# Attention of a four-layer block: the product with V in two halves, and steps of GpSimd, ScalarE and the queues set to other places

## What is computed

```
b, s, _ = x.shape                       # 4, 1024; x is layer-normed before
ids = _adapter_ids(lora_start_indices, b)
Q = _multilora(x, ids, Wq, Aq, Bq)      # x Wᵀ + (x Aᵀ) Bᵀ, by the batch's adapter
K = _multilora(x, ids, Wk, Ak, Bk)
V = _multilora(x, ids, Wv, Av, Bv)
Q, K, V = (split(Q), split(K), split(V))   # 16 heads of 16
Q, K = (_rope(Q), _rope(K))
scores = jnp.einsum('bhqd,bhkd->bhqk', Q, K) / jnp.sqrt(16)
scores = jnp.where(causal, scores, -jnp.inf)
attn = jax.nn.softmax(scores, axis=-1)
out = jnp.einsum('bhqk,bhkd->bhqd', attn, V)
out = out.transpose(0, 2, 1, 3).reshape(b, s, D_MODEL)
return _multilora(out, ids, Wo, Ao, Bo)
```

## Time and profile before

| | us |
|---|---|
| three timed runs | 2107.85, 2112.87, 2113.27 |
| median | 2112.87 |
| the profiled execution, its own time | 2114.4 |
| its span | 2112.7 |
| TensorE, matrix products busy | 1789.8 |
| TensorE, weight loads busy | 1186.0 |
| VectorE busy | 1277.1 |
| ScalarE busy | 864.4 |
| GpSimd busy | 714.8 |

### The profile page before, as it was taken

How to read it: one execution, slowest core, us unless ns; L and a number is a source line. 1 busy time by engine, 2 the same in 40 slices (tenths; PEclk the granted TensorE clock), 3 DMA queues, 4 the chain that set the end, 5 groups by cost and what they waited for, 6 DMA issues and landing times. The chain is left out here.

```text
span 2112.7 us, 30095 instructions
## 1 busy us (share of the span) xinstructions
PE 1789.8 (85%) x9549; PEld 1186.0 (56%) x9549; DVE 1277.1 (60%) x3120; ACT 864.4 (41%) x1791; POOL 714.8 (34%) x873
## 2 busy tenths in 40 slices
PE   5478888889788884799999768989898966999998
PEld 4133333334333333588888635748384745888886
DVE  5476677667676705755555456665766667555554
ACT  2146555556565654122222135553645550222221
POOL 2326344463454421232322123333242321223231
PEclk9669989989997797799999969998999987999999
DMA  5624343342534624376676540110202043767674
GB/s 159 211 66 125 98 140 106 110 132 86 159 97 149 213 80 186 142 259 245 249 255 240 185 175 1 60 41 1 100 1 101 1 181 135 254 240 261 238 258 169
DMA packets 103462, 312.23 MB, mean 148 GB/s; under 512 B 23304, under 2 KB 54796, under 8 KB 93200
## 3 DMA queue, kind: packets, MB, share of 16 engines
q1 hardware_dynamic: 86016, 257.08, 34.5%
q0 software_dynamic: 15936, 50.35, 7.6%
q10 hardware_dynamic: 1360, 2.89, 0.4%
HBM read 245.12 MB, written 53.87 MB: 142 GB/s over the span
## 5 line engine op out<-in xcount | busy, mean ns | idle before, releaser
L772 ACT ACTIVATE a_probs<-a_ps_e 128x512 f32<-128x512 f32 (+3 forms) x768 | 335.9, 491 | 200.8 <-PE a_ps_e L947 196.8
L511 DVE CUSTOM_DVE_ANT_0 a_ps_m<-a_ps_m,a_causal 128x512 f32<-128x512 f32 (+3 forms) x512 | 239.5, 517 | 114.0 <-PE a_ps_m L934 113.1
L1445 ACT CAST hidden_high<-g_ps_h 128x512 fp32r<-128x512 f32 x140 | 75.2, 589 | 400.9 <-PE g_ps_h L1590 400.9
L947 PE MATMUL a_ps_e<-a_q_st,a_k_st 64*128 64x512 f32 (+3 forms) x768 | 185.6, 474 | 60.1 <-ACT a_probs L772 49.0
L947 PEld LDWEIGHTS a_ps_e<-a_q_st,a_k_st 64*128 64x128 f32 x768 | 79.0, 199 | 268.0 <-ACT a_probs L772 190.6
L515 DVE TENSOR_REDUCE a_peak<-a_ps_m 128x1 f32<-128x512 f32 x256 | 164.6, 685 | 102.8 <-PE a_ps_m L934 102.0
L963 PE MATMUL a_ps_a<-a_probs,a_vals 128*32 128x512 f32 (+3 forms) x1536 | 185.9, 560 | 17.3 <-issue 17.1
L934 PE MATMUL a_ps_m<-a_k_st,a_q_st 64*128 64x512 f32 (+3 forms) x768 | 153.5, 401 | 50.1 <-DMA a_k_st<-a_scr_k 23.5
L653 POOL TENSOR_SCALAR_AFFINE_SELECT a_probs<-a_probs 128x256 f32<-128x256 f32 x256 | 103.4, 407 | 270.1 <-ACT a_probs L772 269.1
L111 POOL TENSOR_TENSOR g_xe_rs<-g_xe_ve,table 128x1 f32<-128x1 f32 x70 | 39.3, 561 | 442.9 <-DVE g_xe_ve L1286 442.9
L1578 PE MATMUL g_ps_y<-g_w_d,hidden_high 128*128 128x512 f32 x560 | 143.4, 398 | 5.9 <-DVE x_res L1322 5.9
(11 more groups left out here) (298 smaller groups left out, 3822.8 us busy)
## 6 DMA issues: line engine op xcount, KB each, us to landing
g_w_d<-down_rows SPq DMA_DIRECT2D x70, 2048.0 KB
a_q_st<-a_scr_q POOLq DMA_DIRECT2D x32, 512.0 KB, 4.0
a_k_st<-a_scr_k POOLq DMA_DIRECT2D x32, 512.0 KB, 4.8
m_spread_acs<-m_acs_rows SPq DMA_DIRECT2D x8, 2048.0 KB, 9.6
a_scr_q<-a_high SPq DMA_DIRECT2D x34, 256.0 KB
a_scr_k<-a_high SPq DMA_DIRECT2D x32, 256.0 KB
a_swapped<-a_raw SPq DMA_DIRECT2D x64, 128.0 KB, 2.0
g_x_rows<-x_res SPq DMA_DIRECT2D x8, 1024.0 KB, 12.0
```

What stands on the lines that cost most here:

```text
L511: nc.vector.tensor_tensor_reduce(ps_m[:, bank, 0:w], ps_m[:, bank, 0:w], causal[:, 512 - w:], 1.0, MASKED, ALU.add, ALU.max, peak[:, p % 2 ...
L772: nc.scalar.activation(probs[:, N % RING, r, q0:], ps_e[:, (2 * N + r) % HEAD_BANKS, q0:], ACT.Exp, scale=DH ** -0.5).then_inc(exp_done, 1)
L947: nc.tensor.matmul(ps_e[:, (2 * N + r) % HEAD_BANKS, q0:], k_st[rows(r), p % BUFS, j * P:(j + 1) * P], q_st[rows(r), p % BUFS, 512 * c + q ...
```

## The change

- `weigh` takes a slice of the queries. Where `begin(m)` is under 256 (8 of the 12 entries) the upper half of the queries is done at the even step and the lower half at the odd step behind it. It waits for the masks only where its slice holds the diagonal corner. The other four entries stay whole, at the even step.
- `scale` of the first half goes from step 23 to step 6 of the unit behind it; in the last unit it stays. `scale` of the second half goes from step 13 to 17, `invert` from 7 to 10, `store_inverse` from 8 to 11, `spread_inverse` from 10 to 13.
- `round_high` of the last part of a rope block goes from step 2 to 4, `remainder` from 4 to 5, `keep` from 6 to 8.
- `load` of the first pair of the unit after next goes from step 14 to 13.

```
-                    if U >= 2 and U % 2 == 0 and n == 8:
+                    if U >= 2 and U % 2 == 0 and n == 11:
                         store_inverse(U // 2 - 1, 1)
-                    if U >= 2 and U % 2 == 0 and n == 10:
+                    if U >= 2 and U % 2 == 0 and n == 13:
                         spread_inverse(U // 2 - 1, 1)
...
-                    if U >= 2 and U % 2 == 0 and n == 7:
+                    if U >= 2 and U % 2 == 0 and n == 10:
                         invert(U // 2 - 1, 1)
...
-                    if n == 14 and U + 2 < UNITS:
+                    if n == 13 and U + 2 < UNITS:
                         load(2 * (U + 2))
...
-                    if U % 2 == 1 and n == 23:
+                    if U >= 2 and U % 2 == 0 and n == 6:
+                        scale(U // 2 - 1, 0)
+                    if U == UNITS - 1 and n == 23:
                         scale(U // 2, 0)
-                    if U >= 2 and U % 2 == 0 and n == 13:
+                    if U >= 2 and U % 2 == 0 and n == 17:
                         scale(U // 2 - 1, 1)
...
-            def weigh(U, m):
+            def weigh(U, m, some, last_some):
                 c, j = STEPS[m]
                 b, g = U // GROUPS, U % GROUPS
                 pe.wait_ge(exp_done, 2 * (U * CORE + 2 * m + 2))
-                pe.wait_ge(masked, 2 * (U * sum(DIAG) + sum(DIAG[:m + 1])))
+                if some.start < begin(m) + P:
+                    pe.wait_ge(masked, 2 * (U * sum(DIAG) + sum(DIAG[:m + 1])))
...
-                    last = nc.tensor.matmul(ps_a[32 * u:32 * u + 32, q0:], vals[:, b % 2, j, 17 * h:17 * h + 32],
-                                            probs[:, (U * CORE + 2 * m + u // 2) % RING, u % 2, q0:], start=(j == 0),
-                                            stop=(j == HALF * (c + 1) - 1), tile_position=(0, 32 * u))
-                last.then_inc(pv_done, 1)
+                    last = nc.tensor.matmul(ps_a[32 * u:32 * u + 32, some], vals[:, b % 2, j, 17 * h:17 * h + 32],
+                                            probs[:, (U * CORE + 2 * m + u // 2) % RING, u % 2, some],
+                                            start=(j == 0 and some.stop == 512), stop=(j == HALF * (c + 1) - 1),
+                                            tile_position=(0, 32 * u), skip_group_check=True)
+                if last_some:
+                    last.then_inc(pv_done, 1)
+
+            def weigh_at(M):
+
+                U, m = M // CORE, M % CORE // 2
+                q0, split = begin(m), begin(m) < 256
+                middle = (q0 + 512) // 2
+                if M % 2 == 0:
+                    weigh(U, m, slice(middle if split else q0, 512), not split)
+                elif split:
+                    weigh(U, m, slice(q0, middle), True)
...
-                    if n % 2 == 0 and N >= 4:
-                        weigh((N - 4) // CORE, (N - 4) % CORE // 2)
+                    if N >= 4:
+                        weigh_at(N - 4)
```

More of the change, by code:

```diff
@@ L430, in _ @@
                         keep(sp, 2 * b + 2 + g // 2, (17, 19).index(n))
-                    if g % 2 == 0 and U >= 2 and (U - 1) // GROUPS + 1 < BATCH and n in (3, 6):
-                        keep(sp, (U - 1) // GROUPS * 2 + 2 + (U - 1) % GROUPS // 2, 2 + (3, 6).index(n))
+                    if g % 2 == 0 and U >= 2 and (U - 1) // GROUPS + 1 < BATCH and n in (3, 8):
+                        keep(sp, (U - 1) // GROUPS * 2 + 2 + (U - 1) % GROUPS // 2, 2 + (3, 8).index(n))
                     if n == (22 if g == 0 else 11):
@@ L701, in _ @@
                             remainder(2 * b + 2 + g // 2, i)
-                    if g % 2 == 0 and U >= 2 and (U - 1) // GROUPS + 1 < BATCH and n in (1, 4):
-                        remainder((U - 1) // GROUPS * 2 + 2 + (U - 1) % GROUPS // 2, 2 + (1, 4).index(n))
+                    if g % 2 == 0 and U >= 2 and (U - 1) // GROUPS + 1 < BATCH and n in (1, 5):
+                        remainder((U - 1) // GROUPS * 2 + 2 + (U - 1) % GROUPS // 2, 2 + (1, 5).index(n))
                     for k in range(4):
@@ L821, in _ @@
                         round_high(2 * b + 2 + g // 2, (11, 14, 21).index(n))
-                    if g % 2 == 0 and U >= 2 and (U - 1) // GROUPS + 1 < BATCH and n == 2:
+                    if g % 2 == 0 and U >= 2 and (U - 1) // GROUPS + 1 < BATCH and n == 4:
                         round_high((U - 1) // GROUPS * 2 + 2 + (U - 1) % GROUPS // 2, 3)
@@ L989, in _ @@
                         piece(e)
-                    if n % 2 == 0 and N >= 4:
-                        weigh((N - 4) // CORE, (N - 4) % CORE // 2)
+                    if N >= 4:
+                        weigh_at(N - 4)
                     if N >= 2 and issued_after(N - 2) == TOTAL:
                         keep_warm()
-            for m in (NS - 2, NS - 1):
-                weigh(UNITS - 1, m)
+            for M in range(UNITS * CORE - 4, UNITS * CORE):
+                weigh_at(M)
             for e in LATE:
```

1 line of the change is left out of this document (removed).

## The result

| | us |
|---|---|
| kernel after, four timed runs | 2072.31, 2081.04, 2085.43, 2092.28 |
| median after | 2083.23 |
| median before, beside it | 2113.07 |
| ratio after to before | 0.9862, 95% interval 0.9825 to 0.9899 |
| profiled execution of after, span | 2070.6 |

The forecast was 2055 us, the range 2028 to 2090. The time lies in the range, but 28 us above the forecast and within 1 us of what rival (a) gives. Of the forecast gain of 59 us, 30 came.

What follows compares the result with a forecast made beforehand. TensorE was taken as the nearest bound, with even units losing time to masks held behind GpSimd's scaling wait. Gains of 44 + 4 + 4 + 7 = 59 us from 2114.4 gave 2055 us, range 2028 to 2090.

Steps and rivals of the forecast that it cites:

- rival (a): Attention: gaps before the products with V go, the low clock stays; 30 us gained, about 2084 us; chance 0.12.
- the first scaling: Even units: scaling moved to step 6 frees the masks, removing gaps and low clock behind them; 44 us, ends 17 and 52.
- the halves: Products with V split over even and odd steps: 7 us gained, ends 27 us lost and 46 us gained.
- Rival (d): Even units: the wait only moves, inverses land after step 6, mask of step 7 late; 2099 us; chance 0.04.
- The twins' rule: Units 2, 6 and 10 fall to the lengths of units 3 and 7, which have as many projection pieces: 20.1 us.
- Units 4, 8 and 12, 24 us: Units without twins: gaps of about 8.0 us plus low stretches worth 19, sum of 27 cut to 24.
- Gap + 0.4 x low clock: Gain rule for units 4, 8 and 12: idle gap plus 0.4 of lower-clock time, rate taken from unit 2.
- Rounding, loads, the second scaling: 4 + 4 + 0: Later rope rounding 4 us (ends 0 and 8), sooner loads 4 (ends 0 and 6), second half's later scaling nothing.
- clean pair: Even and odd step without projection pieces: split product shortens the pair from 2.73 to 2.55 us; 14 us in all.
- loaded pairs: Step pairs with 1.9 us pieces on the odd step: each loses about 0.2 us, about 34 pairs lose 7.
- (b): Units 13 and 14: low-clock stretches without a gap go too, 14 us more; 2041 us; chance 0.07.
- (c): Split groups of the products with V cost 0.64 us each, 82 us lost against 52 gained; 2144 us; chance 0.05.

## Why the prediction was right, and where it was wrong

The direction and the wait that it set out to remove were right. That the time lies inside the range is in part luck, since the misses have both signs: the first scaling alone gave 18 of 44 us and the halves -9 for +7, while the other moves, put at 8, gave 18 to 23.

**First scaling.** Right in mechanism: no idle time is left before line 966, and the broadcast waits in even units are gone. Rival (d) is out. The twins' rule was right within 1.2 us (18.9 of 20.1).

**Units 4, 8 and 12, 24 us.** This is the step that failed by most. "Gap + 0.4 x low clock" took the gap before the product with V as what the low clock hangs on, and the rounding's wait as a small thing beside it, 4 us by the 1.22 us of unit 2. With that scaling alone these units gave -0.3, 0.4 and 3.7 us. The rounding's wait stands at the same place, and in these units it was 2.28, 2.29 and 2.65 us before the change already, 7.2 us in sum against 8.0 of gaps. With all moves they gave 5.2, 2.0 and 3.6 us in one profile and 1.4, 2.4 and 2.7 in the other, 6 to 11 in sum: a gap of 1.3 us before the low-rank piece is left in units 4 and 8, one for a load in unit 12, and all three keep stretches at the lower clock. The rate was too high as well: 0.26 to 0.29 us per us at the lower clock from profiles of one kernel, not 0.4. The 4.3 us from which I took it in unit 2 still held the rounding's 1.22; without them it is 3.1 for 10.3 us, 0.30.

**Rounding, loads, the second scaling: 4 + 4 + 0.** Mis-sized together: with the first scaling made, the rest of the moves is worth 18 us by the medians of chips 1 and 2 (2093.97 to 2076.34), 23 by those of chip 1 alone (2093.97 to 2070.89). "I put this at nothing" was wrong for the second scaling. I had named what stands behind it, masks and the output product, and left out the two loads, which the diff itself moves past it. They are what TensorE waits for at step 18 once the rounding is later. By unit lengths, of these 18 to 23 us only 2 to 3 lie in units 5, 9 and 11, for which the sooner load was meant; against the kernel before, these units gave 7 to 8 us, where 5.9 had been read off.

**Halves, +7.** The size of the clean pair was right (0.22 us measured, 0.18 forecast), and so was the loss of loaded pairs (7 us for 30 groups, 7 for 34 forecast). The 14 us of the clean pairs did not reach the end: part of it went to the waits for the maxima and a store, and the 98 halves that are not on loaded steps come with an estimated 5 to 6 us of lower clock, which the forecast had left as it was. So +7 became -9. On the kernel before, where the even units had the most to win, the same halves gave 9.6 us, in part because the upper half does not wait for the late mask, as forecast; once the moves have taken that wait away, this has nothing left to give.

**The rivals.** The time is that of (a), yet (a) is not what happened. It said that gaps go and the low clock stays; the low clock of units 2 and 6 went with the gap, that of 4, 8 and 12 stayed in part (17.1, 13.7 and 23.9 us before, 6.9, 13.6 and 13.7 after). That it gives 2084 is chance: its 17 + 4 + 2 + 7 against 18 + 21 - 9 measured. (b) did not happen. Unit 14 keeps its stretches in every profile (20.5 us after). Unit 13 lost its 17.1 us in the profile after but has 20.5 in the second one of the same kernel, and the moves alone, without any halves, have 3.4 in both: what becomes of it is not the halves' doing. (c) came for the halves in sign, against the moves alone, and where the odd step has a projection its mechanism is there, at 0.23 us a group and not 0.64. Elsewhere it isn't: the pairs are shorter, and steps with two half groups side by side are no longer than with one whole one.

The sum with measured terms: first scaling 18, the other moves 18 to 23, halves -9: 27 to 32, where the change gave 30. The terms are differences of these same kernels, so the sum must come near 30 and proves nothing by itself.

**A change of tiling mode.** Two halves back to back add no change between 64-row and 32-column tiles, and no step of unit 3 grew. At the odd steps each half has two more changes, and the pair of steps 12 and 13 is still shorter by 0.22 us. The Trainium skill ("TensorEngine Tiling (Array Packing)", section "Key Properties") says that a change of mode drains TensorE. No trace here shows a price for a change by itself, and the rule's weight in rival (c) is not borne out.

## What to carry to other kernels

When a wait is moved on an in-order engine, list everything behind it, the transfers it issues too: here moving one scaling behind two loads was worth more (28 us, once the rounding was later) than the wait that the change was aimed at (18 us). Two waits in series at one place look like one; find the second before counting the gap and what follows it. In this kernel levelling shortened the steps where the engine had its next input already, and not beyond, so ask for every shortened step who must now be sooner; and of a change in parts, time the parts, since here leaving the halves out beats both kernels (2070.89 and 2076.34 us, ratio 0.9826 both times).

## What of the hardware was unexpected

What I had read as a group's fixed part was paid once for two groups back to back: 16 records of 256 queries in 1.07 us, as 8 of 512. A broadcast of 256 KB issued right behind three stores of 256 KB each took 8.7 us to land, one issued over 7 us after them 4.2. And one program had 80.5 us of attention at half the clock in one execution and 138.2 in another, the moves alone 67.1 and 95.1, though their instructions are the same: at 0.26 to 0.29 us each, that is 7 to 17 us of time. It differs on one chip, too: the six runs of the whole change beside one another have mean clocks from 0.903 to 0.917.
